# A graph network's four layers on one core: banks written early, group 0's seeds ahead of the small products, later constants behind its row maxima

## The reference

```python
x = _layernorm(x + _L0_gnn_ref(x, adj, adj, ...))  # attention, 8 heads, edge bias
x = _layernorm(x + _L1_gnn_ref(x, adj, ...))       # conv over 17 taps, distances, GRU gates
x = _layernorm(x + _L2_gnn_ref(x, adj, ...))       # additive attention, one head
x = _layernorm(x + _L3_gnn_ref(x, adj, ...))       # graph attention, 4 heads
```

```python
scores = jnp.einsum('bhid,bhjd->bhij', q, k) / math.sqrt(HD) + edge_bias   # edge * W_e[h]
scores = jnp.where(adj_mask[:, None], scores, -jnp.inf)
attn = jax.nn.softmax(scores, axis=-1)
out = jnp.einsum('bhij,bhjd->bhid', attn, v)
```

## Time and profile before

| | |
|---|---|
| median of 3 runs | 1428.95 us (1428.47 to 1429.69) |
| profiled execution | 1432.08 us, span 1430.3 us |
| TensorE busy | 1352.1 us |
| VectorE busy | 1191.3 us |
| ScalarE busy | 1188.4 us |
| GpSimd busy | 663.1 us |
| mean granted clock of TensorE | 0.976 |

### The profile page before, as it was taken

One profiled execution on the slowest core, in us unless ns is written; L12 is line 12 of the kernel. 1 busy time (PEld: TensorE's weight loads), 2 busy tenths in 40 slices (PEclk: granted clock), 3 DMA queues, 4 the chain that ended last, 5 costly groups with the idle time before them and its releaser, 6 DMA issues.

```text
span 1430.3 us, 40514 instructions
## 1 busy us (share of the span) xinstructions
PE 1352.1 (95%) x13178; PEld 1075.1 (75%) x13267; DVE 1191.3 (83%) x3407; ACT 1188.4 (83%) x4353; POOL 663.1 (46%) x1014
## 2 busy tenths in 40 slices
PE   4799999999999999999999999999999999999964
PEld 3577788877778887777888777788877778887642
DVE  6568888888888888888888888888888888886763
ACT  3867888889888888998888899888889988887654
POOL 1133445554444555444455544445554444555532
PEclk7899999999999999999999999999999999999986
DMA  3100110011111001111100111111011111100000
GB/s 117 38 31 31 31 31 17 16 39 38 39 38 39 25 16 39 38 38 39 39 29 12 39 39 38 38 39 34 6 39 39 38 39 38 33 8 16 9 15 23
DMA packets 23825, 46.86 MB, mean 33 GB/s; under 512 B 2753, under 2 KB 2754, under 8 KB 23490
## 3 DMA queue, kind: packets, MB, share of 16 engines
q1 hardware_dynamic: 23618, 44.27, 9.8%
HBM read 35.88 MB, written 8.39 MB: 31 GB/s over the span
## 4 chain that ended last, share of the span: by engine, by line
PE 78%; DVE 10%; POOL 5%; issue 4%; ACT 3%; DVEq 0%; POOLq 0%; ACTq 0%
PE B L591 18%; PE B L689 14%; PE B L499 12%; PE B L537 5%; PE B L558 4%; DVE B L1353 4%; DVE x L1326 3%; POOL rstd L376 3%; PE B L808 2%; PE B L523 2%; PE B L788 2%; PE B L754 2%; PE B L581 2%; PE B L665 2%; PE B L683 2%
## 5 line engine op out<-in xcount | busy, mean ns | idle before, releaser
L995 ACT ACTIVATE e<-B,nm 128x128 f32<-128x128 f32 x1024 | 363.9, 385 | 12.5 <-DVE nm L1361 12.0
L499 PEld LDWEIGHTS B<-ident,e 128*128 128x128 f32 x1536 | 187.0, 144 | 104.3 <-issue 75.7
L499 PE MATMUL B<-ident,e 128*128 128x128 f32 x1536 | 230.0, 281 | 9.2 <-ACT e L1151 3.9
L995 ACT ACTIVATION_READ_ACCUMULATOR e<-B,nm 128x1 f32 x1024 | 231.9, 226 | 0.0
L1353 DVE SCALAR_TENSOR_TENSOR B<-an,rowb,mask 128x512 f32<-128x512 f32 x256 | 194.2, 794 | 19.0 <-ACT pT L1004 9.5
L1151 ACT ACTIVATE e<-l,nm 128x128 f32<-128x128 f32 x512 | 198.9, 400 | 10.0 <-DVE nm L1582 9.9
L1361 DVE TENSOR_REDUCE nm<-B 128x4 f32<-128x512 f32 x256 | 166.5, 683 | 35.0 <-PE B L537 34.8
L1004 ACT ACTIVATE pT<-B 128x512 f32<-128x512 f32 x256 | 157.9, 617 | 44.5 <-PE B L499 41.3
L373 POOL TENSOR_TENSOR veps<-meanv,eps 128x4 f32<-128x4 f32 x128 | 41.8, 326 | 328.9 <-DVE meanv L1320 328.8
L376 POOL TENSOR_TENSOR rstd<-veps,neghalf 128x4 f32<-128x4 f32 x128 | 139.7, 1092 | 10.0
L1582 DVE TENSOR_REDUCE nm<-l 128x4 f32<-128x512 f32 x128 | 87.0, 679 | 41.9 <-ACT l L1141 41.9
(11 more groups left out here) (201 smaller groups left out, 3471.1 us busy)
## 6 DMA issues: line engine op xcount, KB each, us to landing
xt<-in_x_t SPq DMA_DIRECT2D x32, 256.0 KB, 3.1
an<-in_adj_n SPq DMA_DIRECT2D x32, 256.0 KB, 2.7
xn<-in_x_n SPq DMA_DIRECT2D x32, 256.0 KB, 3.3
at<-in_adj_t SPq DMA_DIRECT2D x32, 256.0 KB, 3.2
out_x<-xo SPq DMA_DIRECT2D x32, 256.0 KB, 3.5
wm<-in_mats SPq DMA_DIRECT2D x1, 1088.0 KB, 9.4
wm<-in_mats SPq DMA_DIRECT2D x1, 832.0 KB, 7.1
wm<-in_mats SPq DMA_DIRECT2D x1, 320.0 KB, 3.0
```

The source lines that it names most:

```text
L499: last = mm(g(dst, b), g(src, b), ident[:, :], is_transpose=True, start=(b == 0), stop=True, skip_group_check=True)
L995: last = fn(g(e0[:, h % 2, :], b), g(bank, b), ACT.Exp, bias=nm0[:, h % 4, b:b + 1], accum_out=sum0[s % 2][:, b, head(h):head(h) + 1])
```

## The change

Five things are changed, all in the prologue and in the first group:

- A new constant `flat` (ones, bf16) takes the place of the identity in the bank writes, as GpSimd's first memset. TensorE writes B0, B1 and B3 as its first work, then makes the row product in B2, then writes B5, B6 and B7 and signals `banks_set`. B2 is not written by itself any more: the K projection, a whole bank wide, goes there first.
- The five small products all go to B4 (`SMALL`), into columns of their own. B4 is written whole behind group 0's first scores, and `banks_set` goes to 2.
- VectorE copies the small products out (`small_products`) between the third and the fourth seed of group 0, and then, behind the fourth seed, waits for the second `banks_set`. The first seed waits for the first one.
- `rest_of_weights` stands behind the eighth row maximum of group 0.
- ScalarE starts with a small exponential into a tile `warm`.

```diff
+            def set_bank(i):
+                return mm(B[i][:, :], flat[:, :], flat[:, :].unsqueeze(1).broadcast_to([128, GB, N]), start=True, stop=True)
+            pe.wait_ge(q["flat_set"], 1)
+            for i in (0, 1, 3):
+                set_bank(i)
             pe.wait_ge(q["ones_set"], 1)
             pe.wait_ge(q["wrow"], DMA)
-            mm(B[0][:, 0:NROW], ones[0:1, :], row[:, :], start=True, stop=True).then_inc(q["rows_ps"], 1)
+            mm(B[ROWS][:, 0:NROW], ones[0:1, :], row[:, :], start=True, stop=True).then_inc(q["rows_ps"], 1)
+            for i in (5, 6, 7):
+                last = set_bank(i)
+            last.then_inc(q["banks_set"], 1)
             pe.wait_ge(q["wbb_set"], 1)
-            mm(B[1][:, 0:2], wbb[:, :], col[:, C_A1:C_A2 + 1], start=True, stop=True)
+            mm(small[:, 0:2], wbb[:, :], col[:, C_A1:C_A2 + 1], start=True, stop=True, skip_group_check=True)
...
-            pe.wait_ge(q["pro_read"], 1)
-            pe.wait_ge(q["const_set"], 2)
-            for i in range(8):
-                last = mm(B[i][:, :], identb[:, :], identb[:, :].unsqueeze(1).broadcast_to([128, GB, N]),
-                          start=True, stop=True)
-            last.then_inc(q["banks_set"], 1)
...
@@ project_k
+                if s == 0:
+                    pe.wait_ge(q["rows_read"], 1)
@@ scores
                 last.then_inc(q["qk_ps"], 4)
+                if s == 0 and e == 0:
+                    pe.wait_ge(q["pro_read"], 1)
+                    set_bank(SMALL).then_inc(q["banks_set"], 1)
...
+            act.wait_ge(q["ones_set"], 2)
+            fn(warm[:, :], neghalf[:, :], ACT.Exp)
...
@@ seed_edges
+                if s == 0 and h == 0:
+                    dve.wait_ge(q["banks_set"], 1)
                 v.scalar_tensor_tensor(out=bank[:, :], in0=an[s % 2][:, :], scalar=we[:, head(h):head(h) + 1],
                                        in1=mask0[:, :], op0=ALU.mult, op1=ALU.add).then_inc(q["seed_done"], 1)
+                if s == 0 and h == 2:
+                    small_products()
+                if s == 0 and h == 3:
+                    dve.wait_ge(q["banks_set"], 2)
@@ row_max
+                if s == 0 and h == 7:
+                    rest_of_weights()
...
             for t in range(STEPS):
-                if t == 3:
-                    rest_of_weights()
                 step(t)
```

More of the change, by code:

```diff
@@ L39 @@
 SLOPE = 0.2
+ROWS, SMALL = 2, 4
 NS = 3
@@ L78, in build @@
         att = sb("att", [128, 2, H3])
+        flat = sb("flat", [128, 128], BF16)
+        warm = sb("warm", [128, GB])
         ident = sb("ident", [128, 128])
@@ L193, in build @@
         B = [ps(f"B{i}", [128, W]) for i in range(8)]
-        names = """parity_set wfirst wsecond wtaps wcol wrow ones_set pads_set sel_set id_set const_set bn1_ bn2_ small_set
+        small = B[SMALL]
+        names = """flat_set rows_read parity_set wfirst wsecond wtaps wcol wrow ones_set pads_set sel_set id_set const_set bn1_ bn2_ small_set
             rows_ps att_set wcen_set wbb_set pro_ps diag_set pro_read banks_set prep
@@ L324, in _ @@
         def _(pool):
+            pool.memset(flat[:, :], 1.0).then_inc(q["flat_set"], 1)
             pool.memset(ident[:, :], 0.0).then_inc(q["sel_set"], 1)
@@ L484, in _ @@
             pe.wait_ge(q["att_set"], 1)
-            mm(B[3][:, 0:2 * H3], wm[:, WL3T:WL3T + N], att[:, :, :].rearrange("p a h -> p (a h)"), start=True, stop=True)
+            mm(small[:, 2:2 + 2 * H3], wm[:, WL3T:WL3T + N], att[:, :, :].rearrange("p a h -> p (a h)"),
+               start=False, stop=True, skip_group_check=True)
+            pe.wait_ge(q["diag_set"], 1)
+            mm(small[:, N:2 * N], ones[:, :], diag2[:, :], start=False, stop=True, skip_group_check=True)
             pe.wait_ge(q["wcen_set"], 1)
-            mm(B[4][:, 0:2], wcen[:, :], col[:, C_A1:C_A2 + 1], start=True, stop=True)
+            mm(small[:, 10:12], wcen[:, :], col[:, C_A1:C_A2 + 1], start=False, stop=True, skip_group_check=True)
@@ L488, in _ @@
             pe.wait_ge(q["id_set"], 2)
-            nc.tensor.transpose(B[5][:, 0:N], wcen[:, :], ident[:, :]).then_inc(q["pro_ps"], 1)
-            pe.wait_ge(q["pro_read"], 1)
-            pe.wait_ge(q["const_set"], 2)
-            for i in range(8):
-                last = mm(B[i][:, :], identb[:, :], identb[:, :].unsqueeze(1).broadcast_to([128, GB, N]),
-                          start=True, stop=True)
-            last.then_inc(q["banks_set"], 1)
+            mm(small[:, 2 * N:3 * N], wcen[:, :], ident[:, :], is_transpose=True, start=False, stop=True,
+               skip_group_check=True).then_inc(q["pro_ps"], 1)
@@ L1240, in _ @@
             dve.wait_ge(q["rows_ps"], 1)
-            v.tensor_copy(rowb[:, 0:NROW], B[0][:, 0:NROW]).then_inc(q["small_set"], 1)
+            v.tensor_copy(rowb[:, 0:NROW], B[ROWS][:, 0:NROW]).then_inc(q["rows_read"], 1)
+            dve.wait_ge(q["rows_read"], 1)
             dve.wait_ge(q["bn2_"], 1)
@@ L1248, in _, with small_products @@
             v.tensor_reduce(rmean[:, :], wm[:, WL2N:WL2N + N], AX, ALU.add).then_inc(q["small_set"], 1)
+            dve.wait_ge(q["small_set"], 3)
+            v.tensor_scalar(rmean[:, :], rmean[:, :], 1.0 / N, None, ALU.mult).then_inc(q["small_set"], 1)
             dve.wait_ge(q["small_set"], 4)
-            v.tensor_scalar(rmean[:, :], rmean[:, :], 1.0 / N, None, ALU.mult).then_inc(q["small_set"], 1)
-            dve.wait_ge(q["small_set"], 5)
             v.tensor_scalar(wcen[:, :], wm[:, WL2N:WL2N + N], rmean[:, :], None, ALU.subtract).then_inc(q["wcen_set"], 1)
[L1253 to L1265, removed]
+            def small_products():
+                dve.wait_ge(q["pro_ps"], 1)
+                dve.wait_ge(q["pads_set"], 2)
+                v.tensor_tensor(bl2x[:, 0:1], small[:, 0:1], rowb[:, R_AB:R_AB + 1], ALU.add)
+                v.tensor_copy(bl2x[:, 1:2], small[:, 1:2]).then_inc(q["small_set"], 1)
+                v.tensor_copy(scale2[:, :], small[:, N:2 * N])
+                for j in range(3):
+                    v.tensor_copy(wa2[:, H3 * j:H3 * j + H3], small[:, 2 + H3:2 + 2 * H3])
+                    v.tensor_copy(wa2[:, 12 + H3 * j:12 + H3 * j + H3], small[:, 2:2 + H3])
+                v.tensor_copy(l2w[:, N:HC], small[:, 10:12])
+                dve.wait_ge(q["small_set"], 5)
+                v.tensor_copy(rowb[:, R_AB:R_AB + 2], bl2x[:, :])
+                v.tensor_copy(l2w[:, 0:N], small[:, 2 * N:3 * N]).then_inc(q["pro_read"], 1)
             def rest_of_weights():
@@ L1272, in rest_of_weights @@
                     .then_inc(q["small_set"], 1)
[L1273 removed]
+                dve.wait_ge(q["small_set"], 6)
                 v.tensor_tensor(bnb[:, 0:1], col[:, C_B1:C_B1 + 1], bnt[:, 0:1], ALU.subtract)
                 v.tensor_tensor(bnb[:, 1:2], col[:, C_B2:C_B2 + 1], bnt[:, 1:2], ALU.subtract)
[L1276 removed]
+                dve.wait_ge(q["small_set"], 7)
                 v.tensor_scalar(gb[:, :], gb[:, :], 0.5, None, ALU.mult)
@@ L1301, in rest_of_weights @@
                     .then_inc(q["small_set"], 1)
-                dve.wait_ge(q["small_set"], 12)
+                dve.wait_ge(q["small_set"], 11)
                 taps = wm[:, WC2:WC2 + 16 * N].rearrange("p (c j n) -> p j c n", j=4, n=N)
@@ L1306, in rest_of_weights @@
                 last.then_inc(q["small_set"], 1)
-                dve.wait_ge(q["small_set"], 13)
+                dve.wait_ge(q["small_set"], 12)
                 v.tensor_tensor(wsum[:, 2], wsum[:, 0], wsum[:, 1], ALU.add).then_inc(q["prep"], 1)
```

10 lines of the change are left out of this document (4 added, 6 removed).

## The result

The changed kernel takes 1420.85 us (median of six runs, 1419.17 to 1421.92) against 1429.24 us (six runs, 1428.47 to 1429.69): 8.4 us less, a ratio of 0.994 with a 95% interval from 0.9928 to 0.9952. Timed once more on another occasion it took 1420.56 against 1430.04 us, 0.9935 (0.9922 to 0.9947). The forecast was 1417.1, with a range from 1414.5 to 1420.5, so the direction was right and the time lies 0.35 us outside the range. Of a gain of 11.9 us, 8.4 to 9.5 came.

The account below looks back on a forecast made before the run. Past the fill TensorE was taken as the bound, so only an earlier start counts: 12.73 us earlier first maximum less 0.88 given back is 11.9, taking 1428.95 to 1417.1 us; range 1414.5 to 1420.5.

Parts of the forecast that it names:

- Bank writes: TensorE's start: six writes from about 1.1 us end at 4.85, before VectorE can seed at 6.7, so they cost nothing.
- Small products, K and Q at 0.86 us each: TensorE's prologue: small products end near 7.15, K and Q at the high clock by 8.9, `qT` ready near 9.6 to 9.9.
- Mask and seeds, "VectorE's chain ends last": Group 0 on VectorE: first seed at 6.72, fourth done at 10.70, scores at 10.84, with `qT` ready 1 us before.
- Scores and B4 at the high clock: Group 0 on TensorE: scores 1.17 us, B4's write 0.21, first row maximum at 12.28 instead of 25.01, 12.73 us earlier.
- Rival 1: Low clock at the prologue's end: first maximum near 14.0, gain 10.1 us, 1418.8; only scores slow, 1418.3; chance 28% for both.
- The block behind the maxima: Constants of 7.72 us moved into VectorE's 5.65 us pause before group 1's seeds: gives back 0.88 us.
- The difference to the median is taken over: The profiled execution's time lies 3.1 us above the timed median; the sum keeps that difference, starting from 1428.95.
- The shift arrives at the end: Later groups run the same program, so an earlier first fully busy stretch on TensorE shifts the end of the span.
- rivals 4 and 5: No change, fill's start hidden by something later, 1428.9, 2%; slower, each later group pays, 1435.7 at 0.6 us each, 2%.
- Rival 3: High clock also between the first maxima and group 1's seeds: at most 2.5 us more gain, 1414.6; chance 6%.

Follow-up runs that it names:

- q_bank6: The changed kernel with group 0's Q projected through B6 in place of B1; 1419.83 us, 0.993.
- no_warm: The changed kernel without ScalarE's first small exponential; 1421.58 us, 0.9941.
- after: The changed kernel itself, in its first profile; 1420.85 us, 0.994 of the kernel before.
- after_again: The changed kernel with no edit, for a second profile and five more times; 1420.56 us in the median.
- block_only: The kernel before with only the later layers' constants (`rest_of_weights`) moved behind group 0's eighth row maximum; 1424.66 us, 0.9964.
- before: The kernel without the change, in its first profile; 1429.24 us.
- block_first: The changed kernel with the constants' block put back ahead of group 0's first scores, behind the copies out of B4; 1427.86 us, 0.9987.
- kq_split: The changed kernel with K and Q ahead of the small products and the constants' sums of taps behind group 2's mask; 1417.37 us, 0.9912.
- kq_split_b: The kernel kq_split run a second time with no edit; 1418.77 us, 0.9917.
- split_pool: The kernel kq_split with GpSimd's memset of `xs` held back until group 0's mask is made; 1417.38 us, 0.9911.
- fill_pause: The changed kernel with four more writes of B7 right behind group 0's Q projection; 1420.45 us in the first of two executions.

## Why the prediction was wrong

Going through its own steps:

- *Bank writes*: right. Six are done by 5.1 us and nothing waits for them.
- *Small products, K and Q at 0.86 us each*: this is the step that failed, the high clock put into the sum for K and Q here and for the scores and B4 below. K and Q took 1.71 us each from start to start, the low clock, and `qT` was ready at 10.95, not 9.6 to 9.9. I had seen that the eight writes ran slowly and K fast behind them, and carried the fast K over from one profile. It doesn't hold even in its old place: behind the same eight writes K took 1.02, 1.25 and 1.92 us in three profiles. In the kernel after, 1.8 us of small products stand ahead of K, and it was slow in all seven profiles with that order; that this order is the cause is not shown.
- *Mask and seeds, "VectorE's chain ends last"*: wrong with it. The fourth seed's bank is the one that Q goes through, so `qT` and the seed stand one behind the other, 0.61 us + 0.02 of hand-over + 0.77, where I let both run to the scores side by side. `q_bank6` and `no_warm` show the dependence. In `q_bank6` K and Q were slow too (1.91 and 1.74 us) and delayed nothing: a slow K and Q cost something only through the shared bank. The seeds also began 0.5 us late, at 7.21, because the mask took 0.95 us. So the scores started 1.04 us late, 0.66 of it for `qT` and the rest for the seeds.
- *Scores and B4 at the high clock*: 2.09 and 0.55 us instead of 1.17 and 0.21, the largest part of the miss, 1.22 us. With the 1.04 us above it puts the first maximum at 14.54, 2.26 us late. Rival 1 (28%) had the clock right in all of it and put the maximum at 14.0; it too let `qT` feed the scores past the seed, and came out 0.5 us early. That its 10.1 us is the difference of the two spans is in part luck: the gain was 9.78 us at group 1 and grew by 0.4 us behind it.
- *The block behind the maxima*: 0.88 forecast, 0.69 measured, shown at the low clock by `after`, `after_again` and `block_only` against `before` and `block_first`.
- *"The difference to the median is taken over"*: mis-sized. The sum against the profile missed by 1.8 us (11.9 against 10.1), which alone gives 1418.9, inside the range. The rest, 2.0 us up to the median, is that the profiled execution of before was a long one. A second one was 2.4 us shorter in span, a scatter that the range did not hold. Both errors were needed to leave the range.
- *The shift arrives at the end*: right, so rivals 4 and 5 fall. Rival 3 needed the high clock behind the first maxima; V's projection ran at the low one in both profiles of the kernel after.

Open stays why the same program finds the high clock in one execution and not in the next, and where the smaller steps between executions come from. The Trainium skill, page "TensorE: Matmul & The Clock Gate", section "Part 1: The HAM clock gate", says that the clock's first change comes at another point in each run; `kq_split` and `kq_split_b` agree.

## What to carry to other kernels

When a block leaves the path, follow each input of the next instruction to its own producer and look in which bank or buffer it passes: two chains that look parallel stand in a row if one takes its buffer from the other (here Q's bank and the fourth seed). Don't take the clock of a matmul near the start from one profile (K behind the same bank writes took 1.02, 1.25 and 1.92 us): price it at both levels, and let the range hold both. If the profiled execution lies outside the timed ones, get its excess into the range, since it need not be there in the next. Work that fills a pause costs what it exceeds the pause by, and the pause shrinks when the others get faster: cut the block to the shortest pause.

## What the runs showed of the hardware

The clock column of a profile need not hold before its first change. In the kernel after it reads 1.00 through the first 40 us while K takes 1.92 us, the duration of 0.50 in the earlier trace rows. The same section of "TensorE: Matmul & The Clock Gate" in the Trainium skill warns against trusting the recorded clock events alone; the durations are the check.

VectorE's mask stood behind GpSimd's memset. GpSimd in the kernel after:

```profile
5.79 1.11 POOL L362 MEMSET xs<- 128x1152 f32 x1
```

It ends at 6.90, and the mask that began at 6.23 ended at 7.18, 0.28 us behind it. So it was, with 0.27 or 0.28 us in each, in all seven profiles in which the mask began 0.2 us or more before the memset's end; it took 0.52 to 1.05 us in them. In `q_bank6`, where it began 0.11 us before that end, it took 0.43 us, as it does with no memset beside it (`split_pool`, `fill_pause`). The Trainium skill, page "SBUF — State Buffer", section "SBUF: two separate sides", states that VectorE in its two-port modes and GpSimd take turns on a shared pair of ports, which the one that starts first holds for its whole instruction. These rows agree, though none says in which mode the mask ran, and `split_pool` shows the dependence by an edit: with the memset behind it the mask took 0.43 us.
